# GELU of the cross chunks in two instructions, and the first output tile whole in one step

## The chip, the cores and the metric

The kernel runs on one core of a Trainium2 chip. A core has five engines that run side by side and meet only at semaphores: TensorE (PE), VectorE (DVE), ScalarE (ACT), GpSimd (POOL) and SyncE (SP), which here issues DMAs. The metric is device time in microseconds of one execution; a kernel's time is the median of its runs.

## The reference, cut to what matters

Input x is 2048 x 256, the context 1601 x 192. A first layer routes the context to x and updates it with gates. The second layer is self attention, cross attention and an MLP, each behind a layer norm. What the change touches is the last line but one:

```python
h = _layernorm(x, ln1_g, ln1_b)
x = x + _mha(h, h, sa_wq, ...)
h = _layernorm(x, ln2_g, ln2_b)
x = x + _mha(h, context, ca_wq, ...)          # 16 heads of 16, 1601 keys
h = _layernorm(x, ln3_g, ln3_b)
h = jax.nn.gelu(h @ mlp_w1.T + mlp_b1, approximate=False) @ mlp_w2.T + mlp_b2   # 256 -> 1024 -> 256
return x + h
```

## The kernel before, in words

All tokens are kept in SBUF. Both attentions (a = 0 self, a = 1 cross) work through the queries in four chunks of 512. A chunk runs over 4 groups of 4 heads, and over the key tiles of 128 in each: 13 tiles in the cross attention, so 52 steps a chunk. In step t PE does, in this order: `scores` 2t+2 (two matmuls of 512 columns, L1322, two heads each into two banks of PSUM), `pv` t-1 (four matmuls of 32 columns of weights, side by side, into bank 6, L1339), the small pieces that the step is given, and `scores` 2t+3. ACT turns each pair of score banks into its exponential, one instruction of 128 x 1024 (L897), two to a step. There are three pairs of score banks, so PE can be ahead of ACT by three exps: `scores` n waits until exp n-3 has been counted. `pv` t-1 waits for the two exps of its step.

The pieces are what remains to be done for the chunk before: output projection and residual ("y"), the layer norm's transposes ("h"), the hidden units ("m"), the output tiles ("o"). The table REST gives, for each part of a piece, the step in which it stands; the same table gives the order on DVE, which only takes part in a piece's last part. The pieces share bank 7 of PSUM. Before part 0 of a piece PE waits until DVE has taken the piece before from that bank (`bank7_taken`). In the cross chunks 1, 2 and 3 these pieces are the MLP of chunks 0, 1 and 2; the last chunk's MLP has a tail of its own, which uses other code.

The MLP of a chunk: eight hidden units of 128 x 512 are computed in steps 20 to 35 ("m"), each added to its bias and written to HIDT by DVE (L2009, counted as unit_taken). In step 36, behind its two exps, ACT runs `gelu` over the whole of HIDT in place, 128 x 4096 (L883). Since GELU and exp lie in different function tables, a table load stands on each side. The four output tiles ("o", 128 tokens each) are sums over the eight units, L1421: four parts of two units to a tile. A part is two matmuls of 256 columns in float32, which the profile records as four. DVE adds the bias row (L2014) and the residual (L2017), and POOL issues the store of the tile (L671).

In the table of before, tile 0 has two parts in step 37 and two in step 39, tile 1 two in 42 and two in 43, tile 2 in 45 and 46, tile 3 in 48 and 49. Below, a step with half a tile in it is called heavy, one without light. On DVE the copy of bank 6 at the end of a head group (L1918, `copy_heads`) stands at step 39 too.

Of the kernel before, what the change touches and what calls it, by code (L numbers as in the profile page):

```python
# [11 lines left out]
ACT = mybir.ActivationFunctionType  # L12
AX = mybir.AxisListType.X

P = 128
# [14 lines left out]
HID = 4 * D  # L30
# [36 lines left out]
REST = [  # L67
    {"y": [5, 8, 11, 14], "h": [21, 23], "u": [26, 28, 30, 32], "n": [38, 40]},
    {"y": [5, 7, 9, 11], "h": [17, 18], "m": list(range(20, 28)) + list(range(29, 36)) + [35],
     "o": [37, 37, 39, 39, 42, 42, 43, 43, 45, 45, 46, 46, 48, 48, 49, 49]},  # L70
]

LAST_REST = {"y": [5, 7, 9, 11], "h": [18, 19], "u": [22, 23, 24, 25], "n": [30, 31], "flag": [36], "w1": [42, 45]}
# [42 lines left out]
def wait(eng, s, value):  # L116

    if not isinstance(value, int) or value > 0:
        eng.wait_ge(s, value)
# [12 lines left out]
def build(nc, ctx, d, out):  # L132
# [51 lines left out]
    HIDT = m.put("HIDT", [P, HID // P, CHUNK], F32, oSCR)  # L184
# [56 lines left out]
    def col(name, c=0):  # L241
        i = 2 * COLS.index(name) + c
        return cols[:, i:i + 1]
# [44 lines left out]
    def key_rows(a, kt):  # L288
        return min(P, KEYS[a] - kt * P)
# [387 lines left out]
    def _(act):  # L677
# [198 lines left out]
        for a in range(2):  # L876
            NK, at = NKS[a], A[a]
            steps = GROUPS * NK

            def gelu(q):  # L880

                act.wait_ge(at["unit_taken"], HID // P * (q + 1))
                act.activation(HIDT[:], HIDT[:], ACT.Gelu).then_inc(at["gelu"], 1)  # L883

            def chunk(c, first):
                for t in range(steps):
                    kr = key_rows(a, t % NK)
                    for half in range(2):
                        h = (c * steps + t) * 2 + half
                        act.wait_ge(at["scores"], h + 1)  # L890
                        if half == 0:

                            wait(act, at["pv"], c * steps + t - 1)
                            if a == 1 and first and t < 2:
                                act.wait_ge(A[0]["pv"], CHUNKS * GROUPS * NKS[0] - 1 + t)
                        slot = 2 * ((2 * t + half) % LOOK)
                        act.activation(PX[0:kr, (2 * t + half) % 4, :, :], PS[0:kr, slot:slot + 2, :],  # L897
                                       ACT.Exp, scale=SCALE).then_inc(at["exp"], 1)
                    if a == 1 and t == GELU_STEP and not first:
                        gelu(c - 1)  # L900

            chunk(0, True)
            for c in range(1, CHUNKS):
                chunk(c, False)
            if a == 1:

                q = CHUNKS - 1
                units = HID // P

                def end_scaled(half):  # L910

                    for i in range(2):
                        act.wait_ge(at["hT"], 2 * (q + half) + i + 1)
                        act.activation(HCH[i][:, half * END:(half + 1) * END].bitcast(F32R),
                                       PS[:, END_TURN + i, half * END:(half + 1) * END], ACT.Identity,
                                       scale=col("L1_xattn_ln3_g", i), bias=col("L1_xattn_ln3_b", i))
                        act.activation(HC[:, i, half * END:(half + 1) * END],
                                       PS[:, END_TURN + i, half * END:(half + 1) * END], ACT.Identity,
                                       scale=col("L1_xattn_ln3_g", i), bias=col("L1_xattn_ln3_b", i)) \
                            .then_inc(at["hc"], 1)  # L920

                end_scaled(0)
                act.wait_ge(at["mlp"], q * TPC)
                for n in range(2 * units):
                    half, i = n // units, n % units
                    if n == END_EARLY:
                        end_scaled(1)
                    act.wait_ge(at["unit"], units * q + n + 1)
                    act.activation(HIDT[:, i, half * END:(half + 1) * END],
                                   PS[:, END_HIDDEN[n % len(END_HIDDEN)], 0:END], ACT.Gelu,  # L930
                                   bias=col("L1_xattn_mlp_b1", i)).then_inc(at["unit_taken"], 1)
# [3 lines left out]
    def _(pe):  # L935
        def norm(i, w, bank, halves=range(2)):

            pe.wait_ge(S["squares"], 2 * (i + 1))
            for mm in halves:
                ins = pe.matmul(PS[0:HEADS, bank, 0:w + w % 2], headR[:, mm, :].bitcast(F32R),  # L940
                                SQ[:, mm, 0:w + w % 2].bitcast(F32R), start=(mm == 0), stop=(mm == 1))
            if 1 in halves:
                ins.then_inc(S["norms"], 1)
# [290 lines left out]
        for a in range(2):  # L1234
            NK, at = NKS[a], A[a]
# [129 lines left out]
            def hidden(out_, i, c, span):  # L1365

                w = slice(i * P, (i + 1) * P)
                hi, lo = W1H[c][:, w].bitcast(F32R), W1L[:, c, w].bitcast(F32R)
                h_hi, h_lo = HCH[c][:, span].bitcast(F32R), HCL[:, c, span].bitcast(F32R)
                pe.matmul(out_, hi, h_hi, start=(c == 0), stop=False)  # L1370
                pe.matmul(out_, lo, h_hi, start=False, stop=False)
                return pe.matmul(out_, hi, h_lo, start=False, stop=(c == 1))  # L1372

            def piece(kind, i, q, part, at=at):

                first, last = part == 0, part == PARTS_OF[kind] - 1

                def share(n):

                    w = n // PARTS_OF[kind]  # L1380
                    return range(part * w, (part + 1) * w)

                if kind == "y":

                    if i == 0 and first:
                        pe.wait_ge(at["normed"], (q + 1) * GP)
                        pe.wait_ge(at["wop"], 16)
                    for g in share(GP):
                        ins = pe.matmul(PS[:, 7, 0:D], ONF[:, g, i * P:(i + 1) * P], WOP[:, g, :],  # L1389
                                        start=(g == 0), stop=(g == GP - 1))  # L1390
                    if last:
                        ins.then_inc(at["y"], 1)
                if kind == "h":
                    pe.wait_ge(at["hat"], q + 1)
                    for tt in range(TPC):
                        ins = pe.transpose(PS[:, 7, tt * P:(tt + 1) * P],
                                           XH[:, tt, i * P:(i + 1) * P], ident[:])
                    ins.then_inc(at["hT"], 1)
                if kind == "u":

                    if first:
                        pe.wait_ge(at["hc"], 2 * q + 2)
                    for c in share(2):
                        ins = pe.matmul(PS[:, 7, :], CAWQ[:, c, i * P:(i + 1) * P], HC[:, c, :],  # L1404
                                        start=(c == 0), stop=(c == 1))
                    if last:
                        ins.then_inc(at["unit"], 1)
                if kind == "m":
                    if first:
                        pe.wait_ge(at["hc_lo"], 2 * q + 2)  # L1410
                    for c in share(2):
                        ins = hidden(PS[:, 7, :], i, c, slice(0, CHUNK))
                    if last:
                        ins.then_inc(at["unit"], 1)
                if kind == "n":
                    norm(3 * CHUNKS + q, CHUNK, 7, share(2))
                if kind == "o":
                    if first:
                        pe.wait_ge(at["gelu"], q + 1)
                    for k in share(HID // P):  # L1420
                        ins = pe.matmul(PS[:, 7, 0:D], HIDT[:, k, i * P:(i + 1) * P], W2[:, k, :],  # L1421
                                        start=(k == 0), stop=(k == HID // P - 1))
                    if last:
                        ins.then_inc(at["mlp"], 1)
# [44 lines left out]
            q = CHUNKS - 1  # L1469
# [690 lines left out]
```

## Time and profile before

| | us |
|---|---|
| median of 3 runs | 1500.87 |
| lowest and highest run | 1500.01, 1504.94 |
| the profiled execution | 1502.36 |
| its span, from the first to the last instruction | 1500.7 |
| busy: PE, ACT, DVE | 1397.3 (93%), 1095.9 (73%), 596.3 (40%) |
| mean granted clock of TensorE, 1 is full speed | 0.967 |

The page gives busy time by engine, the chain of work that ended last (followed back from the last instruction, at each step to what released it), and groups of instructions. Busy shares are means over stages that differ; what a change in one place is worth is read from the waits and the chain of that place. Window rows, used below, give for a stretch of time the busy time of each engine with its number of instructions, the granted clock and the share of DMA.

### The profile page before, as it was taken

Reading aid. Unit: us, or ns where it says so; the run is one execution under the profiler, and the core shown is the slowest. Engines: PE = TensorE matmul, PEld = TensorE weight load, DVE = VectorE, ACT = ScalarE, POOL = GpSimd, SP = SyncE. Lnnn points to the kernel's source line nnn. Section 1 sums busy time; section 2 is a strip of 40 time slices with the busy share of each in tenths; the row PEclk is TensorE's granted clock in tenths of the full one; section 3 lists DMA queues with packets and bytes.
Section 4 is the critical chain, followed back from the end, with each engine's and each line's share of the span. In section 5 each row is a group of like instructions: output and inputs, shape, how many; then the busy total and the mean of one; then the engine's idle time right before and its main releaser. Section 6 shows DMA issues by size and latency. Waiting matters only on the chain.

```text
span 1500.7 us, 20741 instructions
## 1 busy us (share of the span) xinstructions
PE 1397.3 (93%) x8014; PEld 635.9 (42%) x8014; DVE 596.3 (40%) x1394; ACT 1095.9 (73%) x1350; POOL 48.7 (3%) x63
## 2 busy tenths in 40 slices
PE   7999989998669999999999999899898999899887
PEld 5667776776422223222322322222233433433346
DVE  5556576676740204312332340343342243144133
ACT  2533435444339999999999999789788797788843
POOL 2000000000010000000000000000000000000000
PEclk9999999998879999999999999899999999999999
DMA  9400001001249200100010353511000000000000
GB/s 305 164 34 1 1 0 57 1 1 57 89 117 126 67 16 19 26 28 11 12 53 12 45 118 47 119 36 35 13 23 15 23 12 12 23 15 1 5 11 15
DMA packets 35048, 66.06 MB, mean 44 GB/s; under 512 B 6202, under 2 KB 20092, under 8 KB 34204
## 3 DMA queue, kind: packets, MB, share of 16 engines
q1 hardware_dynamic: 29580, 43.24, 13.5%
q0 software_dynamic: 5360, 21.37, 3.9%
q8 instruction: 69, 1.13, 0.3%
q14 instruction: 39, 0.32, 0.1%
HBM read 42.70 MB, written 22.02 MB: 43 GB/s over the span
## 4 chain that ended last, share of the span: by engine, by line
PE 68%; ACT 22%; DVE 6%; issue 4%; DMA 1%; DVEq 0%; POOL 0%; SPq 0%; ACTq 0%; POOLq 0%
PE PS L1339 20%; ACT PX L897 20%; PE PS L1322 14%; PE PS L1421 3%; PE PS L1389 2%; PE PS L1139 2%; PE PS L1127 2%; PE PS L1370 2%; PE PS L1130 2%; PE PS L1056 2%; PE PS L1095 2%; PE PS L1096 1%; PE PS L1097 1%; PE PS L960 1%; PE PS L1404 1%
## 5 line engine op out<-in xcount | busy, mean ns | idle before, releaser
L897 ACT ACTIVATE PX<-PS 128x1024 f32<-128x1024 f32 (+1 forms) x928 | 881.7, 1040 | 119.6 <-PE PS L1322 73.3
L1339 PE MATMUL PS<-PX,V 128*32 128x512 f32 (+1 forms) x3712 | 499.3, 610 | 5.0 <-ACT PX L897 3.0
L1322 PE MATMUL PS<-QST,stack 50*128 50x512 f32 (+1 forms) x1856 | 385.5, 472 | 21.8 <-issue 13.5
L1322 PEld LDWEIGHTS PS<-QST,stack 50*128 50x128 f32 (+1 forms) x1856 | 156.8, 185 | 394.6 <-ACT PX L897 327.5
L1918 DVE COPY OT<-PS 128x512 f32<-128x512 f32 x32 | 22.1, 692 | 299.6 <-PE PS L1339 296.0
L1339 PEld LDWEIGHTS PS<-PX,V 128*32 128x32 f32 (+1 forms) x3712 | 73.7, 108 | 150.0 <-issue 111.6
L766 ACT ACTIVATE PH<-PS 128x512 fp32r<-128x512 f32 (+1 forms) x52 | 31.2, 600 | 82.7 <-PE PS L1076 73.2
L1421 PE MATMUL PS<-W,HIDT 128*128 128x256 f32 x192 | 47.8, 392 | 9.7 <-ACT HIDT L883 9.7
L1953 DVE RECIPROCAL REC<-REC 128x256 f32<-128x256 f32 x30 | 52.6, 1753 | 1.0
L782 ACT ACTIVATE TR<-PS,small 128x128 f32<-128x128 f32 x32 | 10.0, 363 | 56.7 <-PE PS L1130 56.7
L1421 PEld LDWEIGHTS PS<-W,HIDT 128*128 128x128 f32 x192 | 34.5, 189 | 33.7 <-issue 30.0
L2009 DVE TENSOR_SCALAR HIDT<-PS,cols 128x512 f32<-128x512 f32 x24 | 18.0, 751 | 74.5 <-PE PS L1372 73.8
L1730 DVE TENSOR_TENSOR PL<-PEXP,PH 128x512 fp32r<-128x512 f32 (+1 forms) x52 | 35.8, 689 | 27.6 <-ACT PEXP L767 26.9
L1095 PE MATMUL PS<-PH,CN 128*128 128x512 f32 (+1 forms) x104 | 44.0, 423 | 0.9 <-DVE PL L1730 0.9
L1982 DVE TENSOR_TENSOR XH<-PS,rows 128x256 f32<-128x256 f32 x28 | 11.9, 425 | 82.0 <-PE PS L1389 82.0
L1096 PE MATMUL PS<-PH,CN 128*128 128x512 f32 (+1 forms) x104 | 42.2, 405 | 0.0
L1097 PE MATMUL PS<-PL,CN 128*128 128x512 f32 (+1 forms) x104 | 42.1, 405 | 0.0
L1622 DVE TENSOR_REDUCE small<-PS 128x1 f32<-128x512 f32 x64 | 35.1, 571 | 10.7 <-PE PS L977 9.8
L1370 PE MATMUL PS<-HCH,W1H 128*128 128x512 f32 (+1 forms) x80 | 33.8, 423 | 3.9 <-DVE HCL L2029 3.9
L2014 DVE TENSOR_TENSOR XH<-PS,rows 128x256 f32<-128x256 f32 x12 | 5.1, 425 | 78.2 <-PE PS L1421 78.2
L1056 PE MATMUL PS<-hF,SAW 128*128 128x512 f32 x64 | 32.1, 638 | 2.0 <-ACT hF L747 2.0
L1370 PEld LDWEIGHTS PS<-HCH,W1H 128*128 128x128 f32 x80 | 15.8, 198 | 42.3 <-issue 20.1
(209 smaller groups left out, 1574.2 us busy)
## 6 DMA issues: line engine op xcount, KB each, us to landing
QST<-q_parts SPq DMA_DIRECT2D x192, 64.0 KB
q_parts<-PARTS POOLq DMA_DIRECT2D x16, 512.0 KB, 3.5
stack<-k_parts SPq DMA_DIRECT2D x24, 200.1 KB, 6.8
stack<-k_parts SPq DMA_DIRECT2D x18, 256.0 KB
k_parts<-KPARTS POOLq DMA_DIRECT2D x8, 512.0 KB, 3.2
v_cross<-V POOLq DMA_DIRECT2D x1, 3328.0 KB, 11.8
V<-v_cross SPq DMA_DIRECT2D x2, 1664.0 KB, 13.6
k_parts<-PARTS POOLq DMA_DIRECT2D x6, 512.0 KB, 3.3
```

The lines of the kernel that those rows point to most:

```text
L897: act.activation(PX[0:kr, (2 * t + half) % 4, :, :], PS[0:kr, slot:slot + 2, :], ACT.Exp, scale=SCALE).then_inc(at["exp"], 1)
L1056: ins = pe.matmul(PS[:, bank, :], SAW[:, "qk".index(kind), c, mm * P:(mm + 1) * P], hF[:, c, at:at + w], start=(c == 0), stop=(c == 1))
L1095: pe.matmul(PS[0:w, bank, :], c_hi, hi, start=first, stop=False)
L1096: pe.matmul(PS[0:w, bank, :], c_lo, hi, start=False, stop=False)
L1097: ins = pe.matmul(PS[0:w, bank, :], c_hi, lo, start=False, stop=last)
L1322: ins = pe.matmul(PS[0:kr, 2 * (n % LOOK) + jj, :], KST[a][lo:lo + NROW, pair, kt * P:kt * P + kr].bitcast(F32R), QST[lo:lo + NROW, pair, ...
L1339: ins = pe.matmul(PS[32 * j:32 * j + 32, 6, :], V[0:kr, kt, 2 * (g // 2 * GH + j) + g % 2, :], PX[0:kr, (2 * t + j // 2) % 4, j % 2, :], s ...
L1370: pe.matmul(out_, hi, h_hi, start=(c == 0), stop=False)
L1421: ins = pe.matmul(PS[:, 7, 0:D], HIDT[:, k, i * P:(i + 1) * P], W2[:, k, :], start=(k == 0), stop=(k == HID // P - 1))
L1622: ve.tensor_reduce(sm(MXP + tt * len(pcs) + p), PS[:, max_bank(m), 0:pcs[p][1]], AX, ALU.max) \
L1730: ve.tensor_tensor(PL[0:kr, n % RING, :].bitcast(F32R), PEXP[0:kr, n % RING, :], PH[0:kr, n % RING, :], ALU.subtract).then_inc(S["l0_lo"], 1)
L1953: ch(ve.reciprocal(part, part))
```

## The change

```diff
 REST = [
...
-     "o": [37, 37, 39, 39, 42, 42, 43, 43, 45, 45, 46, 46, 48, 48, 49, 49]},
+     "o": [37, 37, 37, 37, 39, 39, 41, 41, 43, 43, 45, 45, 47, 47, 49, 49]},
...
             def gelu(q):
 
-                act.wait_ge(at["unit_taken"], HID // P * (q + 1))
-                act.activation(HIDT[:], HIDT[:], ACT.Gelu).then_inc(at["gelu"], 1)
+                w = HID // P // 2
+                for half in range(2):
+                    act.wait_ge(at["unit_taken"], HID // P * q + w * (half + 1))
+                    act.activation(HIDT[:, half * w:(half + 1) * w], HIDT[:, half * w:(half + 1) * w], ACT.Gelu) \
+                        .then_inc(at["gelu"], 1)
...
                 if kind == "o":
-                    if first:
-                        pe.wait_ge(at["gelu"], q + 1)
+                    if part % 2 == 0:
+                        pe.wait_ge(at["gelu"], 2 * q + 1 + part // 2)
```

GELU is issued as two instructions, over units 0 to 3 and over units 4 to 7, and counted twice a chunk. The parts 0 and 1 of an output tile read the first four units, parts 2 and 3 the others; PE waits for the first count ahead of part 0, and for the second ahead of part 2. Tile 0 now stands whole in step 37, and the halves of the other tiles in every second step from 39 to 49. The step of ACT's GELU, 36, is the same, and so is the last step, 49.

ACT at step 36, before: the two exps of the step, the table load, GELU, the table load back, the exps of step 37. PX is the exponentials, PS the PSUM banks.

```order
L897 ACTIVATE PX<-PS 128x1024 [waits cross_pv,cross_scores]
L897 ACTIVATE PX<-PS 128x1024 [waits cross_scores]
L883 ACT_TABLE_LOAD
L883 ACTIVATE HIDT<-HIDT 128x4096 [waits cross_unit_taken]
L897 ACT_TABLE_LOAD [waits cross_pv]
L897 ACTIVATE PX<-PS 128x1024 [waits cross_scores] x2
```

And now:

```order
L900 ACTIVATE PX<-PS 128x1024 [waits cross_pv,cross_scores]
L900 ACTIVATE PX<-PS 128x1024 [waits cross_scores]
L885 ACT_TABLE_LOAD
L885 ACTIVATE HIDT<-HIDT 128x2048 [waits cross_unit_taken] x2
L900 ACT_TABLE_LOAD [waits cross_pv]
L900 ACTIVATE PX<-PS 128x1024 [waits cross_scores] x2
```

One instruction of 4096 columns has become two of 2048, between the same two table loads.

PE at step 37, before: from `pv` 36 (L1339) over the first half of tile 0 (L1421) and scores 77 and 78 (L1322) to `pv` 37. V is the values, W_72 the second weight matrix; cross_unit_taken is the wait for bank 7.

```order
L1339 MATMUL PS<-PX,V 32x512 [waits cross_exp]
L1339 MATMUL PS<-PX,V 32x512 x3
L1421 MATMUL PS<-W_72,HIDT 128x256 [waits cross_gelu,cross_unit_taken]
L1421 MATMUL PS<-W_72,HIDT 128x256 x3
L1322 MATMUL PS<-QST,stack 65x512 [waits cross_exp]
L1322 MATMUL PS<-QST,stack 65x512
L1322 MATMUL PS<-QST,stack 128x512 [waits cross_exp,q_stack1_3]
L1322 MATMUL PS<-QST,stack 128x512
L1339 MATMUL PS<-PX,V 32x512 [waits cross_exp]
L1339 MATMUL PS<-PX,V 32x512 x3
```

And now (the same lines are numbered 3 higher):

```order
L1342 MATMUL PS<-PX,V 32x512 [waits cross_exp]
L1342 MATMUL PS<-PX,V 32x512 x3
L1424 MATMUL PS<-W_72,HIDT 128x256 [waits cross_gelu,cross_unit_taken]
L1424 MATMUL PS<-W_72,HIDT 128x256 x3
L1424 MATMUL PS<-W_72,HIDT 128x256 [waits cross_gelu]
L1424 MATMUL PS<-W_72,HIDT 128x256 x3
L1325 MATMUL PS<-QST,stack 65x512 [waits cross_exp]
L1325 MATMUL PS<-QST,stack 65x512
L1325 MATMUL PS<-QST,stack 128x512 [waits cross_exp,q_stack1_3]
L1325 MATMUL PS<-QST,stack 128x512
L1342 MATMUL PS<-PX,V 32x512 [waits cross_exp]
L1342 MATMUL PS<-PX,V 32x512 x3
```

Two parts have come to stand behind the first two, with a wait of their own for the second count.

PE from `pv` 40, in step 41, before: scores 85 and 86, `pv` 41, and in step 42 the first half of tile 1, which waits for bank 7 (cross_mlp_taken).

```order
L1339 MATMUL PS<-PX,V 32x512 [waits cross_exp]
L1339 MATMUL PS<-PX,V 32x512 x3
L1322 MATMUL PS<-QST,stack 128x512 [waits cross_exp]
L1322 MATMUL PS<-QST,stack 128x512
L1322 MATMUL PS<-QST,stack 128x512 [waits cross_exp]
L1322 MATMUL PS<-QST,stack 128x512
L1339 MATMUL PS<-PX,V 32x512 [waits cross_exp]
L1339 MATMUL PS<-PX,V 32x512 x3
L1421 MATMUL PS<-W_72,HIDT 128x256 [waits cross_gelu,cross_mlp_taken]
L1421 MATMUL PS<-W_72,HIDT 128x256 x3
```

And now, from the same `pv` 40:

```order
L1342 MATMUL PS<-PX,V 32x512 [waits cross_exp]
L1342 MATMUL PS<-PX,V 32x512 x3
L1424 MATMUL PS<-W_72,HIDT 128x256 [waits cross_gelu]
L1424 MATMUL PS<-W_72,HIDT 128x256 x3
L1325 MATMUL PS<-QST,stack 128x512 [waits cross_exp]
L1325 MATMUL PS<-QST,stack 128x512
L1325 MATMUL PS<-QST,stack 128x512 [waits cross_exp]
L1325 MATMUL PS<-QST,stack 128x512
L1342 MATMUL PS<-PX,V 32x512 [waits cross_exp]
L1342 MATMUL PS<-PX,V 32x512 x3
```

The second half of tile 1 stands in step 41, and no part is left in step 42.

## Rows read from the trace of the kernel before

**Rows 1.** The page: its head and the chain that ended last, by engine.

```profile
span 1500.7 us, 20741 instructions
...
PE 68%; ACT 22%; DVE 6%; issue 4%; DMA 1%; DVEq 0%; POOL 0%; SPq 0%; ACTq 0%; POOLq 0%
```

**Rows 2.** Windows: busy us and count by engine, then clock, DMA share, GB/s.

```profile
1092.00:1222.00 130.00, 124.85 (x771) 47.62 (x764) 42.13 (x80) 108.12 (x108) 2.19 (x4) 1.00 0.06 18
```

**Rows 3.** Timeline: start, duration, engine, line, [idle before <-releaser], around GELU of chunk 1.

```profile
1145.15 1.28 ACT L883 ACT_TABLE_LOAD   x1
...
1146.44 3.62 ACT L883 ACTIVATE HIDT<-HIDT 128x4096 f32<-128x4096 f32 x1
...
1150.08 1.28 ACT L897 ACT_TABLE_LOAD   x1
...
1150.21 1.97 PE L1421 MATMUL PS<-W,HIDT 128*128 128x256 f32 x8 [3.25 <-ACT HIDT L883]
...
1151.37 6.56 ACT L897 ACTIVATE PX<-PS 128x1024 f32<-128x1024 f32 x7
...
1152.45 0.44 PE L1322 MATMUL PS<-QST,stack 50*65 50x512 f32 x2 [0.28 <-ACT PX L897]
...
1153.46 0.49 PE L1322 MATMUL PS<-QST,stack 50*128 50x512 f32 x2 [0.57 <-ACT PX L897]
```

**Rows 4.** Line 883, GELU: ns min/median/max, and who waited for it.

```profile
L883 ACT ACTIVATE HIDT<-HIDT x3: 3616/3617/3617, 1146.4 to 1405.8; 128x4096 f32<-128x4096 f32 x3
...
  PE PS L1421: 9.7, 3
```

**Rows 5.** Windows: from GELU's table load to scores 77, chunk 1.

```profile
1145.15:1152.45 7.30, 3.78 (x24) 1.84 (x21) 0.00 (x0) 7.26 (x5) 0.00 (x0) 1.00 0.00 0
```

**Rows 6.** Windows: steps 39 to 49, chunk 1.

```profile
1154.88:1186.94 32.06, 32.03 (x192) 15.22 (x189) 4.12 (x9) 22.66 (x24) 1.65 (x3) 1.00 0.07 22
```

**Rows 7.** The chain in order of time, start, us, in steps 41 to 43.

```profile
1160.90 0.99 PE PS L1339 x8
...
1163.85 1.93 PE PS L1421 x8
...
1165.77 0.66 PE PS L1322 x4
...
1167.43 1.92 PE PS L1421 x8
```

**Rows 8.** Timeline: scores of steps 42, 44, 45 and 46, and one exp.

```profile
1161.83 1.02 PE L1322 MATMUL PS<-QST,stack 50*128 50x512 f32 x4
...
1166.24 1.02 ACT L897 ACTIVATE PX<-PS 128x1024 f32<-128x1024 f32 x1 [1.19 <-PE PS L1322]
...
1169.28 0.74 PE L1322 MATMUL PS<-QST,stack 50*128 50x512 f32 x4
...
1170.95 0.73 PE L1322 MATMUL PS<-QST,stack 50*128 50x512 f32 x4
...
1174.53 0.74 PE L1322 MATMUL PS<-QST,stack 50*128 50x512 f32 x4
```

**Rows 9.** Groups by form, ACT: mean ns; and two in a row in the timeline.

```profile
L721 ACT ACTIVATE CN<-CN 128x2316 fp32r<-128x2316 f32 x1 | 2.1, 2142 | 0.9 <-DMA CN<-in_ctx 0.9
...
L712 ACT ACTIVATE CHI<-ctxT 128x580 fp32r<-128x580 f32 x2 | 1.3, 681 | 0.0
...
15.71 1.26 ACT L712 ACTIVATE CHI<-ctxT 128x580 fp32r<-128x580 f32 x2
```

**Rows 10.** Timeline: DVE in step 39.

```profile
1156.80 0.69 DVE L1918 COPY OT<-PS 128x512 f32<-128x512 f32 x1 [12.30 <-PE PS L1339]
...
1158.70 0.42 DVE L2014 TENSOR_TENSOR XH<-PS,rows 128x256 f32<-128x256 f32 x1 [0.29 <-PE PS L1421]
```

**Rows 11.** Windows, and the timeline of PE, behind the last chunk.

```profile
1452.00:1460.00 8.00, 7.08 (x16) 0.57 0.00 0
...
1452.92 1.22 PE L1359 MATMUL PS<-SUMS,spread 128*128 128x512 f32 x1 [1.70 <-DVE SUMS L1930]
```

## The prediction

> **What bounds the kernel now.** I read the page's chain first: 68% of the time stands with PE and 22% with ACT [rows 1]. Then the windows by stage. Three cross chunks carry the MLP of the chunk before, near 1092 to 1222, 1222 to 1351 and 1351 to 1452; in the first of them PE is busy 124.85 of 130.00 us and ACT 108.12 [rows 2]. So PE sets the pace and what counts is PE's work plus PE's idle time. The reader is to look next for the idle time of PE that is in one piece. The timeline shows it right where the change is [rows 3]: ACT loads the GELU table at 1145.15, runs GELU over all 4096 columns from 1146.44 for 3.62 us, loads the exp table at 1150.08, and gives its next exp from 1151.37. PE has done all it could by 1150.21 - 3.25 = 1146.96 and sits idle for 3.25 us, until GELU ends; then it does the first half of output tile 0 (8 records, 1.97 us) and waits for exp 74, 0.28 us, and for exp 75, 0.57 us. The three chunks are alike: 9.7 us of waiting in 3 times [rows 4]; the 7.30 us from the table load to those scores hold 3.8 us of PE work, and in the other two chunks such a window reads the same [rows 5].
>
> Behind that wait I read how the 11 steps 39 to 49 go, from 1154.88 to 1186.94: 32.06 us with PE busy 32.03 [rows 6] (the windows of the other two chunks give 32.06 as well). ACT is busy only 22.66 us there. The chain in order of time lies on PE from end to end and gives the prices of a step [rows 7]: pv 1.00, two scores 0.66, half an output tile 1.92. A step without half a tile is 1.66 us, a step with one 3.58 us. One step breaks the pattern: step 42, whose scores from 1161.83 take 1.02 us instead of 0.73 [rows 8], because two light steps run ahead of ACT (1.66 us of PE against two exps of 0.94 us each) and PE then waits 0.3 us for an exp. So the 11 steps are 7 x 3.58 + 4 x 1.66 + 0.30 + 0.06 (a longer first scores) = 32.06 us, which is the window.
>
> **The change, part by part.** (1) The second half of tile 0 moves from step 39 to step 37, where PE idles. Heavy steps from 39 on are now 39, 41, 43, 45, 47, 49: six, with five light ones between them, each alone. The stretch becomes 6 x 3.58 + 5 x 1.66 + 0.06 = 29.84 us, 2.22 us less: 1.92 for the half tile and 0.30 for the wait of two light steps in a row, which no longer stand together. That a light step behind a heavy one runs unhindered is shown by step 44 (1169.28 to 1170.95, 1.67 us), and by the heavy step behind it, which takes its 3.58 us (1170.95 to 1174.53) [rows 8]. The last step of the stretch is heavy before and after, so ACT stands as it did when step 50 begins.
>
> (2) Does step 37 hold the added work? The first GELU half: SBUF to SBUF on ACT 2316 columns take 2.142 us and 580 take 0.681 [rows 9], 4096 take 3.617 [rows 4]; the slope between the two long ones is 0.83 ns a column, so 2048 columns take 1.92 us. It ends at 1146.44 + 1.92 = 1148.36; PE starts 0.15 later (as 1150.21 stands to 1150.06 now), at 1148.51, and is done with its 1.92 us at 1150.43. The second half of GELU ends near 1150.18, so PE goes on at once, until 1152.35. Exp 74 ends at about 1152.5, and the scores behind it have to wait for that in any case. The idle 3.25 us shrink to about 1.55, and the step keeps its length, with only 0.15 us to spare.
>
> (3) The second GELU instruction is the cost. It isn't in the trace, so from both sides. Two instructions without any overlap: 2 x 1.92 - 3.62 = 0.22 us. With the overlap that rows show: two activations of 580 columns take 1.26 us together where two of 0.681 would be 1.36, so they overlap by 0.10 [rows 9]; that gives 0.12. The low end is from exps, which read PSUM: one alone takes 1.02 us, and seven in a row 6.56, so each behind the first 0.92 [rows 3, 8]; of that 1024 x 0.83 = 0.85 are columns, which leaves 0.07 for an instruction more. I take 0.12, since the activations of rows 9 read and write SBUF as GELU does. It moves the exp table load and all exps behind it by that much, and until step 39 PE follows ACT (0.57 us of waiting in step 38), so it counts in full. No table load is added: both halves stand between the same two loads.
> The Trainium skill speaks against splitting. "Advanced Engine Details and Errata", The Read-Write Bubble, says that on ScalarE the memory latency shows as a gap between instructions and asks for large tiles. By that rule the halves would not overlap, and the cost would be the upper end, 0.22; the two activations of 580 columns that overlap by 0.10 disagree [rows 9]. By the one the sum is -6.0 us, by the other -6.3.
>
> (4) Waits. PE waits for GELU twice per tile, not once; from the second tile on the count was reached long ago. The step with such a wait (42) and the one without (43) spend the same 1.92 us on the half tile [rows 7], so I book nothing. Part 0 of each tile waits in addition until DVE has taken the tile before from bank 7: that costs DVE 0.42 us [rows 10], and there is a light step of 1.66 us between the end of every tile and the next, before and after. DVE now takes tile 0 at once behind step 37 (near 1152.4, 0.42 + 0.42 us) and only then the copy of pv's bank, which DVE waited 12.30 us for [rows 10]: it isn't late for it, and PE needs that copy only in step 40, with the half tile of step 39 between. Tile 0's store on POOL's queue goes out some 6 us sooner, with nothing behind it. SP's loads for QST are issued as scores finish and are needed a whole chunk later. Nothing else moves.
>
> **The sum** is 3 x (-2.22 + 0.12) = -6.3 us. The profiled execution took 1502.36 us, 1.66 of it outside the span of 1500.7 [rows 1], and would come to 1496.1. It lies 1.5 above the median of the runs, 1500.87, so the forecast for the median is 1494.6 us. A change below 0.3% (4.5 us) can't be told from none here; this one is 0.42%.
>
> **Rivals.**
> No overlap: the first half doesn't get going until GELU is over, by its counts or by how ACT releases them. For it: a margin of 0.15 us is all that step 37 has. Against: the two instructions carry separate counts, and ACT's release took 0.15 us. Then PE has 3.84 us to do from 1150.3, the next scores start at 1154.15, and a step of 1.66 us later step 39 begins at 1155.8 rather than 1154.88. That is 0.95 lost of 2.22: -3.8 us over three chunks, 1497.1.
> ACT hides it: the exps, not PE, set the steps 39 to 49, so that the half tile taken out was free. Then only 3 x 0.12 is left: 1501.2. For it: ACT runs seven exps without a gap just before (1151.37 to 1157.93). Against: ACT idles 1.19 us for the scores behind the half tile of step 42, and much the same behind the other six [rows 8], and is busy 22.66 of 32.06 us [rows 6], and the new stretch of 29.84 still leaves it 7 us.
> Clock, the one that ends slower: TensorE's granted clock is 1.00 through all three waits [rows 5], but near the end it is 0.57 in 1452 to 1460, a mix of its two levels 1.2 and 2.4 GHz, after an idle piece of only 1.70 us [rows 11]. If the new pattern of idle, 2 us of work, and the waits of step 38 drew such a fall behind each GELU, that costs 8 x (1 - 0.57) = 3.4 us each, 10.3 in all, against 6.3 won: +4.0, 1504.9. From two falls of three on, the change doesn't pay. Against it: the wait of 3.25 us drew none, three times of three, and the new idle pieces are shorter.
> The Trainium skill's page "TensorE: Matmul & The Clock Gate", section HAM oscillation, warns of this case, a wait in each round of a loop that throws the array back to the slow clock every time; this trace agrees for the tail alone.
>
> **How the numbers follow.** Forecast 0.87, no overlap 0.05, hidden by ACT 0.05, clock 0.03. Within the forecast the bounds are a gain of 1.92 - 0.22 = 1.70 a chunk (5.1 us, if the 0.30 comes back elsewhere), and 2.22 - 0.07 = 2.15 (6.4 us): 1494.5 to 1495.8; the median of the runs before lies 0.9 above the lowest, so with such a scatter 1493.5 to 1496.7. I leave 0.04 of the 0.87 to a time above 1496.4, the bound of faster. Faster: 0.83; within 0.3%: 0.04 + 0.05 + 0.05 = 0.14; slower: 0.03. The range reaches to the no-overlap case: 1493.2 to 1498.2.
>
> **What would show it.** In the changed profile GELU's line has six records near 1.92 us, its second ending 3.7 us after the first began. PE's idle ahead of the half tile falls from 3.25 to about 1.55 us, and 16 matmul records stand in a row. The exp behind the table load starts 0.1 to 0.2 later than now, counted from the first table load. From step 39's first scores to step 50's, 29.8 us, with no step of scores over 0.8 us in it. From GELU to GELU the distance falls from 129.70 to about 127.6. It would be wrong if the 16 records stood behind the second GELU, if the stretch were near 32 us again with waits for exps in it, if exp 74 started late by more than 0.3 us, or if the granted clock left 1.00 behind a GELU.

## The result, and the profile after

The changed kernel takes 1495.43 us (median of 20 runs, 1488.06 to 1499.21) against 1500.67 for the kernel before in the same jobs (20 runs, 1495.08 to 1505.14). The ratio is 0.9965, with a 95% interval of 0.9953 to 0.9977: 3.5 to 7.1 us faster. The forecast was 1494.6 us and 6.3 us won. Two further comparisons gave 0.9945 [0.9931, 0.9959] and 0.9953 [0.9938, 0.9968].

The head of the page and its chain, which answer to [rows 1]; the execution shown took 1497.27 us:

```profile
span 1495.6 us, 20744 instructions
...
PE 67%; ACT 22%; DVE 6%; issue 3%; DMA 1%; SPq 0%; DVEq 0%; POOL 0%; ACTq 0%; POOLq 0%
```

GELU's line, which answers to [rows 4] (ns min/median/max, first and last start; then who waited):

```profile
L885 ACT ACTIVATE HIDT<-HIDT x6: 1893/1902/1910, 1144.6 to 1404.8; 128x2048 f32<-128x2048 f32 x6
...
  PE PS L1424: 4.6, 3
```

There are six records of 1.90 us, and PE waits for them 4.6 us in three times, not 9.7. The timeline of the second cross chunk, where [rows 3] has the first of before (start, duration, engine, line, idle before and its releaser):

```profile
1271.29 1.28 ACT L885 ACT_TABLE_LOAD   x1
1272.58 3.71 ACT L885 ACTIVATE HIDT<-HIDT 128x2048 f32<-128x2048 f32 x2
...
1274.64 3.70 PE L1424 MATMUL PS<-W,HIDT 128*128 128x256 f32 x16 [1.54 <-ACT HIDT L885]
1276.31 1.28 ACT L900 ACT_TABLE_LOAD   x1
1277.61 6.56 ACT L900 ACTIVATE PX<-PS 128x1024 f32<-128x1024 f32 x7
...
1278.68 0.44 PE L1325 MATMUL PS<-QST,stack 50*65 50x512 f32 x2 [0.34 <-ACT PX L900]
...
1279.69 0.50 PE L1325 MATMUL PS<-QST,stack 50*128 50x512 f32 x2 [0.57 <-ACT PX L900]
```

GELU takes 3.71 us in two instructions, 0.09 more than in one. PE idles 1.54 us instead of 3.25, does all 16 records in a row, and is ready 0.34 us before exp 74. The scores behind come 7.39 us after the table load, where [rows 3] gives 7.30.

Steps 39 to 49, and the stretches behind GELU, in windows (us; busy and count of PE, PEld, DVE, ACT, POOL; granted clock; DMA share, GB/s):

```profile
1143.34:1152.00 8.66, 7.12 (x34) 4.54 (x30) 0.00 (x0) 8.62 (x7) 0.00 (x0) 0.80 0.00 0
1271.29:1280.00 8.71, 6.26 (x36) 3.62 (x32) 0.85 (x2) 8.67 (x7) 0.00 (x0) 1.00 0.00 0
1312.00:1328.00 16.00, 15.05 (x84) 3.93 (x76) 6.83 (x9) 12.15 (x14) 0.54 (x1) 0.79 0.12 34
1153.59:1183.38 29.79, 29.79 (x184) 13.62 (x180) 3.27 (x7) 22.26 (x23) 1.65 (x3) 1.00 0.09 27
```

The stretch that was 32.06 us [rows 6] is 29.79; 29.84 was forecast. But two rows are not at clock 1.00: behind the first chunk's GELU, and where the second chunk passes into the third. That didn't happen in the trace of before: its first chunk reads 1.00 behind GELU and in steps 39 to 49 [rows 5, 6], and its three chunks are alike in the table below. The clearest measure of both effects is DVE's copy of bank 6, four times a chunk and always released by PE. In the trace of before, the copies on both sides of the one at 1156.80 [rows 10]:

```profile
1119.40 0.69 DVE L1918 COPY OT<-PS 128x512 f32<-128x512 f32 x1 [0.93 <-PE PS L1339]
...
1192.00 0.69 DVE L1918 COPY OT<-PS 128x512 f32<-128x512 f32 x1 [4.00 <-PE PS L1339]
```

They lie 37.40 us before it and 35.20 us behind it. In the changed kernel, three neighbours of the first chunk and four of the second:

```profile
1155.45 0.69 DVE L1921 COPY OT<-PS 128x512 f32<-128x512 f32 x1 [2.40 <-PE PS L1342]
...
1188.45 0.69 DVE L1921 COPY OT<-PS 128x512 f32<-128x512 f32 x1 [4.01 <-PE PS L1342]
...
1216.70 0.69 DVE L1921 COPY OT<-PS 128x512 f32<-128x512 f32 x1 [1.13 <-PE PS L1342]
...
1245.54 0.69 DVE L1921 COPY OT<-PS 128x512 f32<-128x512 f32 x1 [0.93 <-PE PS L1342]
...
1283.04 0.69 DVE L1921 COPY OT<-PS 128x512 f32<-128x512 f32 x1 [3.70 <-PE PS L1342]
...
1316.02 0.69 DVE L1921 COPY OT<-PS 128x512 f32<-128x512 f32 x1 [4.01 <-PE PS L1342]
...
1347.14 0.69 DVE L1921 COPY OT<-PS 128x512 f32<-128x512 f32 x1 [1.50 <-PE PS L1342]
```

From step 26 to step 39 the second chunk takes 37.50 us. From the copy in step 39 to that in step 52 they are 33.00 and 32.98 us apart; in the next section 28.25 and, with the clock down, 31.12. In every trace a section of a chunk reads the same to 0.05 us wherever the clock is 1.00, so that kernels can be compared by sections much more finely than by their times. The section with GELU (step 26 to 39) and the one behind it (39 to 52), at clock 1.00, one reading for each kernel with the others within 0.05 us of it, and how many chunks had a fall of the clock from their step 26 on to step 13 of the next:

| kernel | step 26 to 39, us | 39 to 52, us | sum against before | chunks with a fall |
|---|---|---|---|---|
| before | 37.40 | 35.20 | | 0 of 6 |
| split alone | 37.49 | 35.19 | +0.08 | 4 of 6 |
| table alone | 37.88 | 33.00 | -1.72 | 2 of 3 |
| changed | 37.49 | 32.98 | -2.13 | 3 of 9 |
| changed, old spacing | 37.49 | 33.66 | -1.45 | 1 of 3 |
| quarters | 37.69 | 32.98 | -1.93 | 2 of 3 |
| halves, five parts | 37.90 | 32.08 | -2.62 | 0 of 3 |
| quarters, five parts | 37.69 | 32.08 | -2.83 | 0 of 6 |
| quarters, six parts | 38.10 | 31.86 | -2.64 | 0 of 3 |

The two other sections, 28.25 and 28.84 us, are equal in all of them.

### The profile page after: what moved, and what is told of

The parts are those of the page before. It is cut to its first block, busy times and chain, and to the rows that moved or that the text cites. A ratio compares the mean times of both kernels' runs of the same rounds, so it can differ in the third digit from the quotient of the medians.

```text
span 1495.6 us, 20744 instructions
## 1 busy us (share of the span) xinstructions
PE 1395.8 (93%) x8014; PEld 634.1 (42%) x8014; DVE 596.4 (40%) x1394; ACT 1095.8 (73%) x1353; POOL 48.7 (3%) x63
## 4 chain that ended last, share of the span: by engine, by line
PE 67%; ACT 22%; DVE 6%; issue 3%; DMA 1%; SPq 0%; DVEq 0%; POOL 0%; ACTq 0%; POOLq 0%
PE PS L1342 21%; ACT PX L900 20%; PE PS L1325 14%; PE PS L1424 3%; PE PS L1392 2%; PE PS L1130 2%; PE PS L1373 2%; PE PS L1142 2%; PE PS L1133 2%; PE PS L1059 2%; PE PS L1098 2%; PE PS L1099 1%; PE PS L1100 1%; PE PS L1407 1%; PE PS L1375 1%
```

## The experiments

**The split alone.** GELU and its waits as changed, the old table:

```diff
-     "o": [37, 37, 37, 37, 39, 39, 41, 41, 43, 43, 45, 45, 47, 47, 49, 49]},
+     "o": [37, 37, 39, 39, 42, 42, 43, 43, 45, 45, 46, 46, 48, 48, 49, 49]},
```

> GELU in two instructions with the two waits of PE, but the output tiles stand in the steps of the kernel before (37, 37, 39, 39, 42, ...). Theory A (the gain is the half tile that moves out of the stretch of steps 39 to 49, and the split alone buys nothing): PE begins the first half tile near 1.9 us after GELU's start instead of 3.8, but then waits for exp 74, which comes 0.1 us later than before; from GELU's table load to step 39's scores 9.73 becomes 9.82 us, the 11 steps stay 32.06 us, and the time is 0.3 us over before. Theory B (it is the earlier start of PE that pays): each chunk is about 1.7 us shorter, 5 us in all.

Its time was 1509.58 us (6 runs), a ratio of 1.0053 [1.0032, 1.0073], while the trace gave the sections that theory A had named, 37.49 and 35.19, so that B fell. The span of its trace is 7.3 us longer than before's, and the split accounts for 0.3 of it. Another 3.2 us stand in its third chunk, where the clock fell (38.66 and 37.20 us for 37.49 and 35.19), and most of the rest in sections between the two attentions and in the first cross chunk, where the code is the same. The text recorded for the second run overlooked the third chunk. The split alone again:

> The split alone once more. Its first runs lay 8 us over before, while its cross chunks in the trace were only 0.09 us longer each; the rest of the difference stood where its code is that of before, with the granted clock below 1.00 for longer (a mean clock of 0.963). If that was chance of the place and time of these runs, it comes out within 0.3% of before now, with a clock near 0.967. If the split itself does it (theory F, it draws falls of the clock behind GELU), the slow time repeats and the falls stand behind its GELUs.

1508.68 us (12 runs), 1.0031 [1.0011, 1.0052], with a range of 1498.03 to 1513.43. The slow time repeated, and this trace has it inside its chunks: the chunks repeat with 132.94 and 132.91 us where the first trace had 129.79 and 129.77. The timeline of its first chunk:

```profile
1140.21 3.71 ACT L885 ACTIVATE HIDT<-HIDT 128x2048 f32<-128x2048 f32 x2
1142.26 1.97 PE L1424 MATMUL PS<-W,HIDT 128*128 128x256 f32 x8 [1.54 <-ACT HIDT L885]
1143.94 1.28 ACT L900 ACT_TABLE_LOAD   x1
...
1146.31 0.44 PE L1325 MATMUL PS<-QST,stack 50*65 50x512 f32 x2 [2.08 <-ACT PX L900]
...
1147.31 0.50 PE L1325 MATMUL PS<-QST,stack 50*128 50x512 f32 x2 [0.57 <-ACT PX L900]
...
1150.02 1.93 PE L1342 MATMUL PS<-PX,V 65*32 65x512 f32 x8
```

And its windows behind the first and the third GELU:

```profile
1148.00:1156.00 8.00, 8.00 (x32) 3.53 (x24) 1.88 (x4) 3.94 (x5) 0.00 (x0) 0.57 0.16 47
...
1414.00:1422.00 8.00, 8.00 (x32) 3.69 (x24) 2.18 (x5) 3.83 (x5) 0.00 (x0) 0.57 0.01 2
```

PE idles 1.54, 2.08 and 0.57 us with small work between, and then runs about 8 us mostly at 1.2 GHz (0.57 of full speed over the window), at 3.1 us a chunk, in all three chunks; in the first trace in the third only. The split by itself wins nothing. Its 18 timed runs have a mean clock of 0.964 where those of before have 0.966, and both its ratios lie clear above 1: theory F for this kernel, as far as two traces can place the falls.

**The table alone.** The kernel before with the new table; GELU stays one instruction, with its single wait of PE:

```diff
-     "o": [37, 37, 39, 39, 42, 42, 43, 43, 45, 45, 46, 46, 48, 48, 49, 49]},
+     "o": [37, 37, 37, 37, 39, 39, 41, 41, 43, 43, 45, 45, 47, 47, 49, 49]},
```

> The changed table (tile 0 whole in step 37, halves in every second step from 39) with GELU in one instruction, as before. Theory A: PE starts its 3.84 us only behind the whole GELU, so the scores behind come 1.7 us late; ACT's waiting exps take up a part of that, and step 39 begins 10.7 us behind the table load instead of 9.73; the 11 steps take 29.8 us. Net 1.3 us won a chunk, 4 us in all: half to two thirds of the full change. Theory C (the split is not needed, ACT's lead hides all of PE's block): table load to step 39 stays under 9.9 us, and 6.8 us are won, as much as by both.

1498.16 us (12 runs), 0.9978 [0.9964, 0.9992]. The timeline of its first chunk, at clock 1.00:

```profile
1144.90 1.28 ACT L883 ACT_TABLE_LOAD   x1
...
1149.82 1.28 ACT L897 ACT_TABLE_LOAD   x1
1149.95 3.69 PE L1421 MATMUL PS<-W,HIDT 128*128 128x256 f32 x16 [3.25 <-ACT HIDT L883]
1151.12 3.96 ACT L897 ACTIVATE PX<-PS 128x1024 f32<-128x1024 f32 x4
1153.57 0.68 PE L1322 MATMUL PS<-QST,stack 50*65 50x512 f32 x4
...
1155.18 0.72 PE L1322 MATMUL PS<-QST,stack 50*128 50x512 f32 x4
```

PE begins behind the whole GELU, and yet step 39 comes 10.28 us behind the table load at 1144.90, not 10.7, against 9.73 before: scores 77 come 8.67 us behind it, 1.4 us later than before, but ACT has three exps in hand, and step 39 is only 0.55 us late. So the half tile in step 37 costs 0.48 us of the section instead of 1.92 even without any overlap, and 1.72 of the 2.13 us a chunk come from the table. What its time lacks is the clock, which fell behind the second and the third GELU (0.60 and 0.63 over 4 us) and made 37.88 into 39.51 and 39.57.

**The old spacing.** The changed kernel with tiles 1 to 3 where they stood:

```diff
-     "o": [37, 37, 37, 37, 39, 39, 41, 41, 43, 43, 45, 45, 47, 47, 49, 49]},
+     "o": [37, 37, 37, 37, 42, 42, 43, 43, 45, 45, 46, 46, 48, 48, 49, 49]},
```

> The changed kernel, but tiles 1 to 3 keep their steps of before (42, 42, 43, 43, 45, 45, 46, 46, 48, 48, 49, 49), so that steps 38 to 41 are four light ones in a row. Theory A with the term of 0.3 us for light steps in a row: a light step behind another is paced by ACT's two exps (1.87 us, not 1.66), the 11 steps take 30.4 to 30.7 us instead of 29.8, and 2 to 2.5 us over three chunks are given back. Theory D (spacing is of no account, only the number of heavy steps): 29.8 us.

The section reads 33.66 us against 32.98: 0.68 a chunk, 2.0 in all, at the low edge of the 2 to 2.5 us that theory A had (its 11 steps would be 30.5). The time was 1498.33 us (12 runs), 0.9983 [0.9968, 0.9997], 2.9 us above the changed kernel's median and 4.9 above its median in the same job; this trace has a fall of its own in one chunk. PE in the light steps in a row:

```profile
1281.05 0.97 PE L1325 MATMUL PS<-QST,stack 50*128 50x512 f32 x4
...
1283.09 0.76 PE L1325 MATMUL PS<-QST,stack 50*128 50x512 f32 x4
...
1284.78 0.99 PE L1325 MATMUL PS<-QST,stack 50*128 50x512 f32 x4
```

The scores of steps 40 and 42 are drawn out to 0.97 and 0.99 us by waits for exps. Spacing counts; theory D falls.

**The changed kernel again,** twice, unedited:

> The changed kernel as it is, for another trace and more times. In the first one TensorE's granted clock was 0.59 in the 4 us behind the first GELU half of one chunk, and 0.83 in 20 us near the end of another; the steps of the kernel before kept 1.00 in all its cross chunks. If such falls come at random in either kernel, this trace has them elsewhere or not at all, and windows at 1.00 read 29.79 us for the 11 steps and 9.82 from table load to step 39. If the change calls them up, one of the three windows behind GELU is below 1.00 again. The time is 5 to 6.5 us below before.

1493.42 us (6 runs); the table's sections, no fall behind GELU, one at the same boundary as in the first trace (28.25 us became 31.12).

> The changed kernel once more, beside the next ones. Where the clock is 1.00, 37.49, 32.98, 28.25 and 28.84 us from head sum to head sum; 5 to 6.5 us under before. A third trace tells if its cross chunks have falls of the clock again (two, and one, in the two so far; none in two traces of before).

1495.74 us (12 runs), and no fall in the cross chunks of this trace: they repeat with 127.56 and 127.58 us, against 129.69 and 129.70.

**The kernel before against itself,** unedited:

> The kernel before as it is, against itself: what a comparison of two equal kernels shows here, and where its clock falls this time. Theory A: from one copy of the head sums to the next the cross chunks read 37.40, 35.19, 28.25 and 28.84 us wherever the granted clock is 1.00, and the ratio is 1 within 0.3%. Theory E (falls of the clock come by chance in any kernel, where PE has been idle for a while): one or two falls inside the cross chunks in this trace, which had none the first time. Theory F (the change draws them): again none.

0.9993 [0.9975, 1.0011]. Again no fall in its three cross chunks. Earlier in the program this trace has two sections longer than the first trace of before, 34.61 us for 32.37 and 28.21 for 26.66, with the code the same. So such falls differ between executions of the same code; whether the change adds some of its own in the cross chunks is not settled by 3 of 9 against 0 of 6, since the chunks of one execution fare alike too often to count one by one.

**GELU in quarters.** Four instructions of two units, a wait for every part, the changed table:

```diff
-                w = HID // P // 2
-                for half in range(2):
+                w = HID // P // 4
+                for half in range(4):
...
-                    if part % 2 == 0:
-                        pe.wait_ge(at["gelu"], 2 * q + 1 + part // 2)
+                    if True:
+                        pe.wait_ge(at["gelu"], 4 * q + 1 + part)
```

> The changed kernel with GELU in four instructions of two units and a wait of PE for each part. The second instruction cost 0.09 us in the traces, so two more cost 0.18 a chunk: table load to step 39 is 10.0 us instead of 9.82, the 11 steps stay 29.79, and the time is 0.5 us over the changed kernel's, though PE begins tile 0 almost 1 us sooner. Rival (PE's early start is worth something by itself): the chunks get 0.4 us shorter or more.

At clock 1.00 the section is 37.69 us, 0.20 above halves, as expected, so PE's early start is worth nothing by itself. The time is 1501.75 us (12 runs, 1.0001 [0.9982, 1.0019]), 6 us above the changed kernel. In its trace PE is done with tile 0 early and idles 1.21 us for exp 74, and the clock falls in the second and third chunk:

```profile
1278.53 0.45 PE L1325 MATMUL PS<-QST,stack 50*65 50x512 f32 x2 [1.21 <-ACT PX L900]
...
1280.10 1.93 PE L1342 MATMUL PS<-PX,V 128*32 128x512 f32 x8
```

The 8 records of pv take 1.93 us there instead of 1.06.

**A fifth part in step 37.** In the changed kernel, a quarter of tile 1 behind tile 0:

```diff
-     "o": [37, 37, 37, 37, 39, 39, 41, 41, 43, 43, 45, 45, 47, 47, 49, 49]},
+     "o": [37, 37, 37, 37, 37, 39, 39, 41, 43, 43, 45, 45, 47, 47, 49, 49]},
```

> The changed kernel, and a quarter of tile 1 (two units, 0.96 us) moved from the 11 steps into step 37 as well, behind tile 0: o is 37 five times, 39, 39, 41, then as before. The quarter has to wait some 0.6 us for DVE to take tile 0 from bank 7; scores 77 come 1.3 us later, of which ACT's three exps in hand take up all but 0.4 to 0.5. The stretch from step 39 to 50 is 28.85 us instead of 29.79, table load to step 39 near 10.3 instead of 9.82: 0.45 us won a chunk, 1.4 us under the changed kernel. Rival (ACT has nothing in hand, what is put in step 37 is paid in full): step 39 begins 1.3 us or more later and nothing is won.

37.90 and 32.08 us (32.13 in the two other chunks): 0.44 to 0.49 a chunk below the changed kernel, for 0.45 expected. 1493.42 us (6 runs), 0.9941 [0.9919, 0.9963], which the times alone can't tell from the changed kernel.

**Quarters and five parts,** both edits, run twice:

> GELU in four instructions and the quarter of tile 1 in step 37 (both edits together). PE is done with tile 0 about 0.7 us sooner than with halves, so the quarter ends before exp 75 and step 39 begins near 10.0 us behind the table load; the 11 steps take 28.85 us. Per chunk 0.75 us under the changed kernel, 2.3 us in all, which would make it the fastest of all. Rival: as in the kernel with halves, no better (DVE's wait and the exps behind the fourth GELU instruction take it back).

> GELU in quarters and five parts in step 37, again: 37.69 and 32.08 us at clock 1.00, so 0.7 us a chunk or 2.1 us under the changed kernel in the same job.

1493.52 us (11 runs), 0.9949 [0.9930, 0.9968], and 1490.12 us (6 runs), 0.9919 [0.9897, 0.9942]. The sections say 0.70 a chunk below the changed kernel, 2.1 us in all, for 2.3 expected. The timeline of one chunk:

```profile
1142.25 3.90 ACT L885 ACTIVATE HIDT<-HIDT 128x1024 f32<-128x1024 f32 x4
1143.45 3.88 PE L1424 MATMUL PS<-W,HIDT 128*128 128x256 f32 x16 [0.69 <-ACT HIDT L885]
...
1147.91 1.13 PE L1424 MATMUL PS<-W,HIDT 128*128 128x256 f32 x4 [0.59 <-DVE XH L2017]
1148.98 1.06 PE L1325 MATMUL PS<-QST,stack 50*65 50x512 f32 x4
```

Quarters alone lose 0.20; with work behind tile 0 to use the time that they free, they win. The idle pieces of PE are down to 0.69 and 0.59 us, and no trace of this kernel has a fall in its chunks. It beats the kernel before in both jobs. Against the changed kernel the ratios' intervals overlap, a little in the second job (0.9938 to 0.9968 for the changed kernel); but there 11 of its 12 runs are slower than the slowest of these 6, and the sections at clock 1.00 agree. In the other job the changed kernel wasn't run.

**Six parts,** half of tile 1 in step 37, quarters in most other steps:

```diff
-     "o": [37, 37, 37, 37, 37, 39, 39, 41, 43, 43, 45, 45, 47, 47, 49, 49]},
+     "o": [37, 37, 37, 37, 37, 37, 39, 39, 41, 42, 43, 44, 46, 47, 48, 49]},
```

> As the one with quarters and five parts, with half of tile 1 in step 37 and the other ten parts at 39, 39, 41, 42, 43, 44, 46, 47, 48, 49. One more part of 0.92 us leaves the 11 steps; scores 77 come 1 us later, and ACT's exps in hand (until 9.5 us behind the table load) still cover that but for 0.4 to 0.5. The two sections 37.69 and 32.08 become about 38.15 and 31.15: 0.5 us a chunk, 1.4 us under the one with five. Rival: what ACT has in hand is used up, the sixth part is paid in full, no gain.

38.10 us as expected, but 31.86 where 31.15 were: nothing won over five parts (1493.46 us, 7 runs, 0.9943 [0.9922, 0.9964]). PE at the first step with a quarter alone:

```profile
1157.51 0.72 PE L1325 MATMUL PS<-QST,stack 50*128 50x512 f32 x4
1158.16 1.06 PE L1342 MATMUL PS<-PX,V 128*32 128x512 f32 x8
1159.16 1.13 PE L1424 MATMUL PS<-W,HIDT 128*128 128x256 f32 x4
1160.22 0.73 PE L1325 MATMUL PS<-QST,stack 50*128 50x512 f32 x4
```

From 1159.16 to 1160.22 a quarter holds PE for 1.06 us, not for half of 1.92. Eight steps with a quarter alone pay that 0.1 us eight times. What was expected of ACT was right; the price of a part was not. The 0.7 us by which the section misses 31.15 are close to these 0.8.

## Why the prediction was right or wrong

1. The stretch: right in all its terms. 29.79 us measured for 29.84; the term for light steps in a row is shown by the old spacing, which gives back 0.68 where four stand together.
2. Step 37 holds the added work: right. The wait of 1.54 us (1.55 forecast) and exp 74 still the later one, with 0.34 us to spare instead of 0.15, because 16 records in a row take 3.70 us and not twice 1.92.
3. The second instruction: 0.09 us, between the chosen 0.12 and the low end, 0.07. Two records of 1.902 us are 3.80 us in a sum and take 3.71 together, so the two overlap by 0.09. The Trainium skill ("Advanced Engine Details and Errata", The Read-Write Bubble) has memory accesses pipelined within an instruction but not between instructions, by which they would not overlap; this trace disagrees.
4. Waits: right, no half tile took longer, and DVE had tile 0 out of the bank in time (2.40 to 3.70 us of waiting still ahead of the copy, from 12.30).
5. The sum: 2.13 us a chunk at clock 1.00 for 2.10 forecast, 6.4 in all for 6.3. The medians show 5.2 and the trace after only 5.1 of span (1500.7 to 1495.6). Its chunks had two falls, 0.37 us in the section with GELU and 2.87 at the boundary; the rest is 1.8 us less before the first GELU (1143.34 for 1145.15), where the code is the same, and 0.2 in the tail. So it is luck that this one trace comes so near to the medians. The sum had no term for falls of the clock: in the three traces of the changed kernel they cost 6.1 us of its chunks' time, 2.0 an execution, and in the two of before nothing. Whether that is the 1.1 us between the forecast and the median isn't shown.
6. The rival "no overlap" was mis-sized, because it took a late start of the scores as paid in full, with ACT's three exps in hand left out; and with it my view of what the gain is made of. I priced a late start of PE at 0.95 us a chunk, the second instruction included; the table alone shows 0.48, and 0.57 with the 0.09 of that instruction. Overlap with GELU is worth 0.41 of the 2.13 us a chunk (1.72 without), and alone, with no work moved into the gap, it costs 0.08. The work that moved is what counts, into a place where ACT is ahead.
7. The rival of the clock stood at 3% and named a fall behind each GELU at 3.4 us. For the changed kernel it failed: one fall behind nine GELUs, at 0.37 us, and mean clocks over its runs (0.968) no lower than before (0.966). Still, that one fall is a thing the prediction had named as a sign of being wrong, and the two larger ones, 2.87 us each, stand some 40 us behind the second GELU; whether the change has a part in them is open. And what the rival described is found next door: four falls of 3.1 to 3.2 us with the split alone, for 3.4 in the prediction. The Trainium skill's "TensorE: Matmul & The Clock Gate", HAM oscillation, describes a loop whose wait in each round throws the array back to the slow clock each time. The second trace of the split alone looks like that, three times of three; the first, with the same waits, has it once in three. I had argued that shorter idle pieces are safer, and that argument doesn't hold: several of 1.54, 2.08 and 0.57 us close together were followed by falls in 4 of 6 chunks, 3.25 us, with 0.28 and 0.57 us behind it, in none of 6. That rests on two executions of each kernel.

## What to carry to other kernels

When an engine waits for a long instruction of another, ask first which work can be moved behind that wait so that the other engine's buffered input covers it; splitting the instruction is the smaller part, and is a loss if nothing fills the time. When a few microseconds decide, compare sections between recurring instructions of the trace that are at the same granted clock, and look at the idle pieces of PE that a change leaves behind, not at their sum. Keep the pieces put between other matmuls large.

## What the runs showed of the hardware that was not expected

- Runs of one kernel on one core spread by 12 us (1495 to 1507 for the kernel before), and the spread goes with the mean granted clock: a line fitted through the more than 200 timed runs here that have a clock, each kernel with a level of its own, has 0.001 of clock go with about 1.1 us and leaves 1.4 us of scatter. From the first of the copies of bank 6 on, at 469 to 476 us, traces of equal code differ by more than 0.05 us a section only where the clock is below 1.00.
- Three idle pieces of 1.54, 2.08 and 0.57 us with small work between them were followed by 8 us mostly at 1.2 GHz (0.57 of full speed) in 4 of 6 chunks; one of 3.25 us was followed by no fall in 6 chunks with a half tile behind it, and by 4 us at 0.60 and 0.63 in 2 of 3 with a whole tile. What decides it is open. The chunks of an execution tend to fare alike, so their place in time may be part of it; this wasn't tried.
- A piece of n float32 matmul records of 256 columns between other matmuls holds PE for 1.06, 1.92 and 3.62 us at n = 4, 8 and 16: an estimate from the three is 0.21 us a record and 0.2 for the piece.
- On ACT, SBUF to SBUF, GELU over 4096 columns takes 3.62, 3.71 and 3.90 us in one, two and four instructions: some 0.09 us for each more.
